# A five-layer graph network kernel: block sums kept in PSUM, per-octet counters, packed spans and paired stack loads

## The reference: what is computed

```python
# 1: five layers l
h_in = h + vn[batch]
emsg = relu(h_in[src] + edge_attr @ We[l] + be[l])
t    = h_in + segment_sum(emsg, dst)
t    = relu(t @ W1[l] + b1[l]) @ W2[l] + b2[l]       # then batch norm; relu but for the last layer
h    = t + h_in                                       # and a small update of vn
# 2: weighted graph convolution
out  = segment_sum(x[src] * edge_weight, dst) @ W_rel.T + b_rel + x @ W_root.T   # batch norm, relu, + x, relu
# 3: attention over the edges of each node, 8 heads
# 4: three graph convolutions
h    = segment_sum(norm * (h @ W)[src], dst) + b      # with self loops, relu after the first two
```

## Time and profile before

| quantity | value |
|---|---|
| median of three executions | 9692.08 us |
| profiled execution, its own time | 9716.49 us |
| its span, first to last instruction | 9714.7 us |
| mean granted TensorE clock | 0.796 of full |
| PE busy | 5983.3 us (62%) |
| POOL busy | 5129.5 us (53%) |
| DVE busy | 3648.9 us (38%) |
| ACT busy | 1871.5 us (19%) |
| instructions | 125184 |

### The profile page before, as it was taken

The page is one execution under the profiler, slowest core; times in us unless marked ns, Lnnn a source line. Parts: engine busy times, 40 slices in busy tenths (PEclk is TensorE's granted clock), DMA queues, the critical chain, the costliest instruction groups (busy, mean ns, idle before and its releaser), DMA issues. The chain is left out here.

```text
span 9714.7 us, 125184 instructions
## 1 busy us (share of the span) xinstructions
PE 5983.3 (62%) x28184; PEld 4631.5 (48%) x28185; DVE 3648.9 (38%) x6033; ACT 1871.5 (19%) x4127; POOL 5129.5 (53%) x5128
## 2 busy tenths in 40 slices
PE   3667656665676667657765573556665565556556
PEld 2455545554555455445644462444443453444345
DVE  4444433443344334434431224445551231222123
ACT  1222211121112112212222233333330000000000
POOL 4544365446554655555556644444316665665666
PEclk8888878887888789878977786777786786777677
DMA  4322333233333333333332224554423232332332
GB/s 122 96 89 89 94 104 95 88 94 104 92 91 95 107 94 94 98 100 102 98 93 84 79 59 160 195 182 164 144 87 89 87 88 82 88 88 77 91 94 86
DMA packets 434336, 986.60 MB, mean 102 GB/s; under 512 B 125952, under 2 KB 210432, under 8 KB 417536
## 3 DMA queue, kind: packets, MB, share of 16 engines
q0 software_dynamic: 245760, 673.51, 23.9%
q1 hardware_dynamic: 130864, 194.89, 6.3%
q10 hardware_dynamic: 57296, 114.45, 3.5%
HBM read 844.97 MB, written 137.49 MB: 101 GB/s over the span
## 5 line engine op out<-in xcount | busy, mean ns | idle before, releaser
L335 POOL DMA_INDIRECT ring<-node_table,idx x4608 | 4611.3, 1001 | 3747.2 <-issue 1813.1
L990 DVE TENSOR_TENSOR ring<-ring,psE 128x1024 f32<-128x1024 f32 x640 | 759.6, 1218 | 861.6 <-issue 570.1
L1403 POOL DMA_INDIRECT ring<-att_table,idx x512 | 517.4, 1010 | 766.3 <-ACT idx L1607 494.9
L1115 PE MATMUL psE<-ring,shared 128*128 128x256 f32 x2304 | 722.6, 462 | 281.1 <-issue 193.8
L843 ACT ACTIVATE ring<-ring 128x1024 f32<-128x1024 f32 x640 | 664.4, 1054 | 1194.2 <-DVE ring L990 742.2
L914 DVE TENSOR_TENSOR AGG<-AGG,psAT x480 | 201.9, 421 | 1664.8 <-remote 950.4
L661 PE MATMUL psE<-we_stk,stk 128*128 128x256 bf16 x2560 | 402.4, 296 | 554.6 <-DVE ring L990 243.6
L1115 PEld LDWEIGHTS psE<-ring,shared 128*128 128x128 f32 x2304 | 505.8, 229 | 489.5 <-issue 335.3
L736 PE MATMUL psAT<-ring,S 128*128 128x256 f32 x2560 | 653.0, 410 | 97.4 <-issue 51.9
L736 PE MATMUL psAT<-ring,shared 128*128 128x256 f32 x2560 | 659.2, 413 | 87.2 <-issue 56.2
L1230 DVE TENSOR_TENSOR AGG<-AGG,psE x288 | 120.8, 420 | 1353.7 <-remote 874.9
(11 more groups left out here) (351 smaller groups left out, 8359.4 us busy)
## 6 DMA issues: line engine op xcount, KB each, us to landing
ring<-node_table,idx POOLq DMA_INDIRECT x4608
rows_table<-ring SPq DMA_DIRECT2D x64, 1072.0 KB
ring<-rows_table ACTq DMA_DIRECT2D x64, 1072.0 KB
stk<-stack_table SPq DMA_DIRECT2D x256, 256.0 KB
node_table<-tab ACTq DMA_DIRECT2D x237, 128.0 KB, 1.9
stack_table<-stk SPq DMA_DIRECT2D x64, 256.0 KB
ring<-att_table,idx POOLq DMA_INDIRECT x512
tT<-in_edge_attr SPq DMA_DIRECT2D x68, 64.0 KB
```

Of the source, the lines that this page charges most:

```text
L335: nc.gpsimd.indirect_dma_start(ring[:, q, 0:gw], None, table, bass.IndirectOffsetOnAxis(ap=idx[:, q:q + 1], axis=0)).then_inc(gathered[q], 16)
L990: nc.vector.tensor_tensor(ring[:, q:q + 4, 0:D], ring[:, q:q + 4, 0:D], psE[:, D * u:D * u + 4 * D].rearrange("p (u f) -> p u f", u=4), AL ...
L1115: ins = nc.tensor.matmul(bank, S_first[ob][:, u, :], ring[:, U * ob + u, 0:D], start=(u == 0), stop=(u == U - 1))
L1403: nc.gpsimd.indirect_dma_start(ring[:, U * (ob % 2) + u, 0:GW], None, att_table, bass.IndirectOffsetOnAxis(ap=idx[:, q:q + 1], axis=0)).th ...
```

## The change

It touches all passes but attention.

- **Sums stay in PSUM.** A block's octets now accumulate in one bank (`start=False`); `open_sums` clears the bank's state once by a small matmul. The unit of a further block goes to the other of two banks. DVE adds the bank to `AGG` once for a block instead of once for a unit. In the message and weighted passes `take_sums` writes `tin` straight from `AGG` and the bank, and then `AGG`. DVE waits for `first_done` or `row_done` before it writes the next one-hot: in the message passes this is the unit before, in the others three units earlier.
- **Octet counters.** Semaphores now count octets, with increments of 1; thresholds are registers that are stepped by 1. `encoded`, `added` and `message` are split in halves of an octet.
- **Packed spans.** The further blocks of four octets are packed in one word (`further_row`), read once for four octets; block numbers are kept by counting. `further` stands once in DVE's loop.
- **Indices** for four octets are copied at once, into two alternating halves of `idx`; in the weighted and convolution passes ACT waits for `row_done` of the turn before.
- **Stacks** are loaded two at a time.
- **Weighted pass:** DVE, not ACT, multiplies by the edge weights, four slots in one instruction.
- In the first message pass the two halves of an octet are taken in the other order. The first octet's block is taken as 0, the last one's by counting. The attention pass keeps its work; one of its semaphores starts higher.

The core of the diff:

```diff
+        def first_unit(pe, ob, hots, bank, ready, done, frees, order=range(U)):
+            for t, u in enumerate(order):
+                ready(u)
+                ins = nc.tensor.matmul(bank, hots[:, u, :], ring[:, U * ob + u, 0:D],
+                                       start=False, stop=True, skip_group_check=True)
+                if t == 0 and frees:
+                    ins.then_inc(octet_free, 1)
+            ins.then_inc(done, 1)
+        def further_unit(pe, ob, hots, tile):
+            other_bank(pe, bank_pe)
+            bank = sums_in(tile, pe, bank_pe)
+            pe.wait_ge(sums_read, ng_pe)
+            pe.wait_ge(hot_further, ng_pe)
+            for u in range(U):
+                ins = nc.tensor.matmul(bank, hots(u), ring[:, U * ob + u, 0:D],
+                                       start=(u == 0), stop=True, skip_group_check=True)
+            ins.then_inc(further_done, 1)
...
+        def next_indices(i):
+            j = nc.s_assert_within((i + 1) & (NG - 1), 0, NG - 1, ...)
+            half = nc.s_assert_within((i + 1) & 1, 0, 1, ...)
+            nc.scalar.copy(idx[:, bass.ds(half * RING, RING)], src_i[:, bass.ds(j * RING, RING)]
+                           ).then_inc(idx_ready, OB)
...
             def load_stacks(sp):
                 with sp.Fori(0, NG) as i:
-                    for ob in range(OB):
-                        o = NO * l + OB * i + ob
-                        sp.wait_ge(encoded, U * (o + 1))
-                        sp.dma_start(stk[:, ob, :], stack_table[bass.ds((OB * i + ob) * P, P), :]
-                                     ).then_inc(stk_in[ob], 16)
+                    for p in range(2):
+                        sp.wait_ge(encoded[0], at_sp)
+                        sp.wait_ge(encoded[1], at_sp)
+                        sp.dma_start(stk[:, 2 * p:2 * p + 2, :], stack_table[...]).then_inc(pair_in[p], 16)
+                        sp.reg_add(at_sp, at_sp, 2)
...
 message_pass, DVE, for each octet:
-                            lo, cnt = (dve.snap(reg) for reg in now_dve[0])
-                            then = span_of(dve, octet_behind(h))
+                            cnt = further[ob]()
...
-                            c = dve.snap(nd)
-                            add_sums(c - U).then_inc(unit_added, U)
-                            dve.reg_add(nd, nd, U)
-                            hot_unit(hot_sets[(ob + 1) % 2], octet_behind(h), then[0]).then_inc(hot_first, 1)
+                            dve.wait_ge(first_done, at_dve)
+                            hot_unit(hot_sets[(ob + 1) % 2], octet_behind(h), then).then_inc(hot_first, 1)
...
+                                    dve.wait_ge(further_done, nd)
+                                    further_hots(h, c)
+                                    dve.wait_ge(first_done, at_dve)
+                                    take_sums(n, b, bank).then_inc(sums_read, 1)
+                                    scaled(n)
+                                    dve.drain()
+                                    finish(n, ...)
...
 weighted_pass, ACT and DVE, for each octet:
-                            for q in range(U * ob, U * ob + U):
-                                act.wait_ge(gathered[q], 16 * (NG * k + i + 1))
-                                nc.scalar.activation(ring[:, q, 0:D], ring[:, q, 0:D], ACT.Copy,
-                                                     scale=weight[:, bass.ds(RING * i + q, 1)]).then_inc(message, 1)
+                            for g in range(2):
+                                q = U * ob + 4 * g
+                                for t in range(q, q + 4):
+                                    dve.wait_ge(gathered[t], landed)
+                                nc.vector.tensor_tensor(
+                                    ring[:, q:q + 4, 0:D], ring[:, q:q + 4, 0:D],
+                                    weight[:, bass.ds(RING * i + q, 4)].unsqueeze(2).to_broadcast([P, 4, D]),
+                                    ALU.mult).then_inc(row_weighed[g], 1)
...
 conv_pass, ACT, for each turn of four octets:
+                        act.wait_ge(row_done, at_act)
+                        next_indices(i)
```

More of the change, by code:

```diff
@@ L562, in _ @@
-                    add_sums(c - U)
+                            cnt = further[ob]()
+                            then = block_on(dve, last_blk, cnt)
+                            dve.wait_ge(row_done, at_dve)
+                            hot_unit(S_first[(ob + 1) % OB], octet_behind(h), then).then_inc(row_hot, 1)
+                            for g in range(2):
[6 more added lines that the diff above has]
+                                    ALU.mult).then_inc(row_weighed[g], 1)
@@ L755, in _, with ready @@
-                            first_unit()
-                            with pe.If(cnt > 1):
-                                with pe.Fori(1, cnt):
+                            def ready(u):
+                                if u == 4 * halves[0]:
+                                    pe.wait_ge(hot_first, at_pe)
+                                if u % 4 == 0:
+                                    pe.wait_ge(message[u // 4], at_pe)
+                            first_unit(pe, ob, hot_sets[ob % 2], sums_in(psAT, pe, bank_pe), ready, first_done, False,
+                                       [4 * g + u for g in halves for u in range(4)])
@@ L978, in _ @@
                         for ob in range(OB):
                             h = OB * i + ob
-                            o = NO * l + h
-                            lo, cnt = (dve.snap(reg) for reg in now_dve[0])
-                            then = span_of(dve, octet_behind(h))
-                            for u in range(0, U, 4):
-                                q = U * ob + u
+                            cnt = further[ob]()
+                            for g in halves:
+                                q = U * ob + 4 * g
@@ L993, in _ @@
                                 if l == 0:
-                                    if u == 0:
+                                    if g == halves[0]:
                                         dve.wait_ge(stk_turned, h + 2)
                                         dve.wait_ge(stk_in[(ob + AHEAD) % OB], 16 * (i + 1))
-                                    for step in range(2) if u == 0 else range(2, SPLIT):
+                                    for step in range(2) if g == halves[0] else range(2, SPLIT):
@@ L1031, in _ @@
[L1031 to L1040 removed]
+                            then = block_on(dve, last_blk, cnt) if ob < OB - 1 else block_or_first(dve, last_blk, cnt, i)
@@ L1041, in _ @@
                     n = dve.snap(nf_dve)
+                    b, bank = block_at(dve, last_blk), sums_in(psAT, dve, bank_dve)
+                    dve.wait_ge(first_done, at_dve)
+                    dve.wait_ge(further_done, nd)
+                    take_sums(n, b, bank)
                     scaled(n)
-                    add_sums(c - U)
                     dve.drain()
-                    put_in(n, last())
                     finish(n, a_block(dve.snap(done_dve[1])), a_block(dve.snap(done_dve[2])))
@@ new lines, in _ @@
+                            first_unit(pe, ob, S_first[ob], sums_in(psE, pe, bank_pe), ready, row_done, True)
+                            pe.reg_add(at_pe, at_pe, 1)
+                            cnt = further[ob]()
+                            with pe.If(cnt > 0):
+                                with pe.Fori(0, cnt):
+                                    m = pe.snap(nf_pe)
+                                    further_unit(pe, ob, lambda u: S_further[:, u, :], psE)
+                                    if not final:
+                                        turn(m)
+                                        result(m)
+                                    pe.reg_add(nf_pe, nf_pe, 1)
@@ L1158, in _ @@
                     pe.reg_add(nf_pe, nf_pe, 2)
+                    if not final:
+                        pe.sem_inc(row_done, 1)
                 @block.scalar
@@ L1313, in _ @@
                     m = dve.snap(nf_dve)
-                    add_sums(c - U)
+                    b, bank = block_at(dve, last_blk), sums_in(psE, dve, bank_dve)
+                    dve.wait_ge(row_done, dve.snap(at_dve) + (OB - 2))
+                    dve.wait_ge(further_done, nd)
+                    add_sums(b, bank)
                     dve.drain()
```

615 lines of the change are left out of this document (272 added, 343 removed).

## The result

The changed kernel took 9627.59 us in the median (9583.53 to 9643.96), the kernel before 9693.08 us beside it. The ratio is 0.9926, 95% interval 0.9901 to 0.9950: 0.74% or some 70 us less. The forecast was 9240 us, 450 us less. The profiled execution took 9627.59 us with a span of 9625.8, so 88.9 us of span are gone against the profile of before.

The account below looks back on a forecast made before the run. The prediction took POOL's gathers as the pace, held up by the loop over DVE, ACT and PE. Terms of 100 + 80 + 120 + 50 + 100 = 450 us off 9716.5, less 24.4 to the median, gave 9240 us; range 8800 to 9640.

Parts of the forecast that it names:

- first rival: Waits only change their names: some 150 us less in all, 9542 us, range 9450 to 9670; chance 0.22.
- What bounds the kernel: POOL would be the bound if it didn't pause; its 1860.6 us of waits come from the loop over DVE, ACT, PE.
- (e): Weighted and convolution passes: DVE waits for a unit three back, halving POOL's 219.4 us of waits; 100 us less.
- (a): Indices of four octets copied at once: half of POOL's 209.6 us wait behind ACT's copy goes, 100 us less.
- (b): PE reads the span word once in four octets, cutting 108.1 us of issue before L736; 80 us less.
- (c): DVE reads fewer words, drops address arithmetic, holds `further` once: a third of 342 us at its loop's end, 120 us less.
- (d): Message passes: DVE loses 480 adds and about 160 copies, gains two adds for each of 160 blocks; 50 us less.
- (f): Weighted pass: multiplying by weights moves from ACT to DVE, adding 156 us there; cost 0 if POOL stays the pace.
- (g): SP loads stacks in pairs, half as many loads, with the earlier octet's lead falling from four octets to three; 0.
- third rival: Paired stack loads arrive late and PE waits for them: slower, 9795 us, range 9711 to 9950; chance 0.09.
- The loop's end: DVE idles 4.27 us at the end of a loop body, 342 us over 80 turns; instruction fetch a possible cause.
- fourth rival: The gap at DVE's loop end goes wholly, 342 instead of 120 us: 9020 us, range 8950 to 9090; chance 0.07.

## Why the prediction was wrong, step by step

The sign held, and the wide range held by only 12 us of its upper end; the size did not: some 70 us instead of 450. The first rival (waits only change their names, 9450 to 9670) is what happened, and it had 0.22. Its own figure was off as well: a third of the terms a to d, 350 us, is 117 and not 150, and even that was more than came.

- **What bounds the kernel.** The rows were read rightly: PE's results are acted on late while gathers stream. The failing step is the next one. Having seen that, the sum still priced the work on the loop (registers, adds, indices) as if it lay on the path. It lies beside the wait for PE. The parts put back show it: the words and the add, forecast at 1.5 to 2.6%, gave 0.6% less time, the closer wait of (e), forecast at 1.0%, 0.3% less, and the index copies of (a), forecast at 1.0%, 0.1% more, each known to some 0.4%.
- **(a) Indices, 100 us.** The wait behind ACT's copy went as foreseen, and POOL's named waits for PE did not rise either; what came in their place stands under "issue" (321 us before the fifth octet of every eight). Put back octet by octet, the copies make POOL wait 737.2 us behind ACT and cost nothing that can be told. The sentence "soon waits for a free octet" points the right way, and half was too much.
- **(b) PE's word, 80 us.** The issue time before L736 was forecast at 27 us and is 55.1 + 51.6 = 106.7 against 108.1: these gaps were not the reading of the word. PE reads one in four words now, and the gaps stayed. The row was ascribed to a cause that it did not show.
- **(c) DVE's scalars, 120 us.** The idle time fell as forecast (168.6, under 300) and came back as a wait for `encode`, and as issue before the one-hots: 515.7 us after, 393.7 us before, in the line
```profile
DVE shared L261 <- issue: 393.7, 192, 13.7
```
  Of these the words were put back on DVE too, at no cost; the address arithmetic was not put back.
- **(d) Adds, 50 us.** The counts were right, 160 pairs in place of 480. One add and a drain for each octet put back cost nothing.
- **(e) Decoupling, 100 us.** POOL's waits behind the units of these passes were not halved: 262.6 us after, 219.4 before. The last convolution is 20 us shorter, and yet the closer wait put back costs nothing that can be told.
- **(f) Weights, 0.** Right in the sum. DVE rose to 390 us, 420 was foreseen. Wrong in a reason: I took it from the attention pass that the product doesn't get in the way of the gathers. The Trainium skill, "SBUF — State Buffer", section "Who interferes with whom", says that a DVE instruction with two SBUF inputs contends with a GpSimd instruction that reads SBUF. The weighted pass agrees with it by 52 us. The attention pass agrees as well: I read its mean of 1.01 us, in which the 30 gathers beside a product hardly count.
- **(g) Stacks, 0.** Right: single loads put back make no difference, and the third rival did not occur.
- **The loop's end.** DVE's issue before L990 shrank by 401.5 us; before the first L990 of each of the 80 turns alone it went from 271 to 85 us, and the instruction queue of the whole kernel moved 1.15 MB instead of 3.07. The Trainium skill, "Runtime: NRT & Kernel Launch", section "Instruction fetch mechanics", says that a taken branch to a target outside the current two-page window must first fetch it. The trace agrees for a body without a second `further`; which part of it is the branch, which the words, no run separates. The fourth rival's 342 us did not come: the time turned into waiting.

**What stays open.** No single part that was put back gives up the 70 us; each ratio is known to some 0.3% and each difference to some 0.4%, so the gain may be several small ones, or lie in what was not put back (the accumulation in PSUM itself, the counters, the single `further`). How POOL's issuing holds PE up was not settled either: the records fit a PE that truly advances slowly (records 1.4 to 2.1 us apart) and a PE whose reports are slow. And no run spaced the gathers evenly instead of stopping after some of them, so whether the length of the stop or the rate of the gathers counts is open too.

## What to carry to other kernels

Before pricing work off an engine, ask whether that engine waits right behind it for something that the work does not move; then the saving turns into waiting. Compare the idle time of the pacing engine as a whole, since waits change their names. And where one engine streams gathers, try a short stop at a natural boundary: it costs one line, and here it was worth more than six times the change (4.9% against 0.7%). Its length and spacing have to be tried: a stop after every four gathers made the kernel 10% slower than no stop.

## What the runs showed of the hardware

- While gathers were issued back to back 1.25 us apart, a result of PE was acted on 15.8 us after its last record; over four message passes one case in ten was over 21.7 us, and with a stop of 2.7 us for every eight gathers 8.0 us. A stop of about 1.4 us for every eight gathers made the kernel 4.9% faster than without, one of 2.7 us 2.1%, next to none 1.0%.
- It does not go by bytes or rows: 256 B rows instead of 1 KB changed nothing (0.9900), and 16 rows instead of 128, which brings the gathers 0.1 us closer together, cost 2.9% against the changed kernel.
- A gather of 16 rows takes 902 ns and one of 128 rows 1005 ns.
- DVE's products of two SBUF operands lengthened the gathers of the weighted pass from 1.00 to 1.10 us on the mean. The gathers that lay mostly beside such a product took 1.52 us, the others 0.97.
